# GRU, attention, RK4 and FP8 FFN on one core: small start loads, FFN input transposes in slot nine of sixteen, GpSimd's tail work on VectorE

## The reference

```python
def reference(x, cond, ...):
    h = gru(initial=cond, inputs=x, W_ih, W_hh, b_ih, b_hh)    # 64 steps, one after the other
    x = x + attention(layernorm(h) * gamma, Wq, Wkv, Wo)       # 16 heads of 128, one k/v head, rotary, causal
    q = rk4(q0=cond, p0=cond, drive=x, coupling, bias)         # 64 steps of 4 stages each
    return x + ffn(q, w_gate, w_up, w_down)                    # 512 -> 1408 -> 512, FP8 grid, row scales

def gru_cell(h, x):
    i_r, i_z, i_n = split(x @ W_ih + b_ih, 3)
    h_r, h_z, h_n = split(h @ W_hh + b_hh, 3)
    r, z = sigmoid(i_r + h_r), sigmoid(i_z + h_z)
    n = tanh(i_n + r * h_n)
    return (1 - z) * n + z * h

def derivative(q, p, drive):                                   # four of them to an RK4 step
    return q - q**3 / 3 - p + drive + tanh(q) @ coupling.T + bias, EPSILON * (q + ALPHA - BETA * p)
```

## Time and profile before

| | |
|---|---|
| median of three runs | 1656.17 us |
| the profiled execution, its own time | 1656.58 us |
| its span | 1654.7 us |
| mean granted TensorE clock | 0.978 of full |
| busy: TensorE, weight loads, VectorE, ScalarE, GpSimd | 90%, 56%, 68%, 35%, 24% |
| chain that ended last: TensorE, VectorE, idle, ScalarE, DMA, GpSimd | 74%, 11%, 6%, 5%, 2%, 2% |
| DMA, issue to landing: W_ih and W_hh (3 MB each) | 10.4 and 13.5 us |
| DMA, issue to landing: the first xT (64 KB), x rows (256 KB) | 1.8 and 2.7 us |

### The profile page before, as it was taken

One profiled execution on the slowest core, in us unless ns is written; L12 is line 12 of the kernel. 1 busy time (PEld: TensorE's weight loads), 2 busy tenths in 40 slices (PEclk: granted clock), 3 DMA queues, 4 the chain that ended last, 5 costly groups with the idle time before them and its releaser, 6 DMA issues.

```text
span 1654.7 us, 46345 instructions
## 1 busy us (share of the span) xinstructions
PE 1491.5 (90%) x16582; PEld 930.7 (56%) x16623; DVE 1122.2 (68%) x3561; ACT 587.3 (35%) x1902; POOL 400.2 (24%) x554
## 2 busy tenths in 40 slices
PE   5999999997699999999999996788888888888884
PEld 2333333336576766757576744566666666666652
DVE  2676777766674756556474714578888888888885
ACT  2444444541202021110202012445555555555552
POOL 0222211210000000000000001245555555555554
PEclk9999999998899999999999998999999999999997
DMA  7111112116000000000000032001111111111111
GB/s 293 47 51 46 44 49 73 57 26 175 1 1 26 0 25 2 24 6 19 25 0 25 0 127 102 24 27 36 36 37 33 33 32 35 32 37 42 35 34 33
DMA packets 90692, 72.44 MB, mean 44 GB/s; under 512 B 32472, under 2 KB 82824, under 8 KB 89608
## 3 DMA queue, kind: packets, MB, share of 16 engines
q1 hardware_dynamic: 71128, 59.38, 12.0%
q10 hardware_dynamic: 17744, 6.49, 1.6%
q0 software_dynamic: 1760, 5.77, 1.2%
HBM read 54.66 MB, written 16.94 MB: 43 GB/s over the span
## 4 chain that ended last, share of the span: by engine, by line
PE 74%; DVE 11%; issue 6%; ACT 5%; DMA 2%; POOL 2%; SPq 1%; DVEq 0%; POOLq 0%; ACTq 0%
PE ps L659 13%; PE ps L649 13%; PE ps L754 12%; PE ps L587 10%; PE ps L597 10%; PE ps L693 3%; PE ps L744 3%; PE ps L717 3%; ACT mem L962 2%; DVE mem L1283 2%; DVE mem L1325 2%; ACT ps L954 2%; PE ps L768 1%; PE ps L670 1%; DVE ps L1293 1%
## 5 line engine op out<-in xcount | busy, mean ns | idle before, releaser
L754 PE MATMUL ps<-mem 128*32 128x128 f32 x8192 | 282.1, 279 | 81.4 <-ACT mem L962 78.4
L754 PEld LDWEIGHTS ps<-mem 128*32 128x32 f32 x8192 | 214.3, 111 | 156.6 <-ACT mem L962 109.1
L649 PE MATMUL ps<-mem 128*128 128x512 f32 x512 | 224.6, 592 | 0.0
L659 PE MATMUL ps<-mem 128*128 128x256 f32 x1024 | 222.3, 379 | 0.0
L659 PEld LDWEIGHTS ps<-mem 128*128 128x128 f32 x1024 | 193.9, 190 | 26.0
L512 POOL TENSOR_TENSOR mem<-mem 128x128 f32<-128x128 f32 x64 | 30.9, 483 | 731.2 <-ACT mem L957 731.2
L587 PE MATMUL ps<-mem 128*32 128x384 f32 x2048 | 179.7, 492 | 0.7 <-DMA mem<-in_xT 0.7
L597 PE MATMUL ps<-mem 128*32 128x384 f32 x2048 | 177.6, 487 | 2.4 <-DVE mem L1110 2.4
L929 ACT ACTIVATE mem<-mem 128x512 f32<-128x512 f32 x32 | 19.7, 630 | 390.9 <-DVE mem L1223 390.9
L649 PEld LDWEIGHTS ps<-mem 128*128 128x128 f32 x512 | 95.6, 190 | 109.7 <-issue 109.3
L962 ACT ACTIVATE mem<-mem 128x64 f32<-128x64 f32 x512 | 102.7, 248 | 116.4 <-DVE mem L1283 116.3
(11 more groups left out here) (141 smaller groups left out, 2110.8 us busy)
## 6 DMA issues: line engine op xcount, KB each, us to landing
mem<-x_scr SPq DMA_DIRECT2D x128, 64.0 KB, 1.8
mem<-in_xT SPq DMA_DIRECT2D x64, 64.0 KB, 2.0
mem<-in_Wq SPq DMA_DIRECT2D x1, 4096.0 KB
mem<-in_Wo SPq DMA_DIRECT2D x1, 4096.0 KB, 20.8
mem<-in_x SPq DMA_DIRECT2D x16, 256.0 KB, 2.7
x_scr<-mem SPq DMA_DIRECT2D x32, 128.0 KB, 2.3
q_scr<-mem SPq DMA_DIRECT2D x64, 64.0 KB, 1.6
mem<-q_scr SPq DMA_DIRECT2D x64, 64.0 KB, 1.9
```

The source lines that it names most:

```text
L649: mm = pe.matmul(ps[:, 6 + pr, :], aoT[:, h, pr * P:pr * P + P], wo[:, h, :], start=(h == 0), stop=(h == HEADS - 1))
L659: mm = pe.matmul(ps[:, h % Q_BANKS, 0:BLK], wq[:, c, h * DH:(h + 1) * DH], xnb[:, c, :], start=(c == 0), stop=(c == NC - 1))
L754: mm = pe.matmul(ps[32 * j:32 * j + 32, st % 2, 0:P], thT[:, c, :], ct[:, c, j * P:(j + 1) * P], start=False, stop=(c == NC - 1), skip_gro ...
```

## The change

Start: the biases are prepared on the host for all 128 partitions and loaded by two DMAs on ScalarE's queue (256 and 128 KB). VectorE adds the second to two thirds of the first. TensorE makes one product into each of banks 0 and 1, ScalarE then writes the biases over them. SP loads xT, cond and the state first, waits for the bias loads, then loads W_ih and W_hh, the latter in two halves with a semaphore each. The copy of the identity on ScalarE moves behind the first pair of GRU steps.

Groups: TensorE's transposes of the FFN input move from slot 10 to slot 9 (the tenth).

Tail: in groups 16 to 18 VectorE does what GpSimd did, except for the gate's scale. The residual rows of tile 15 are loaded early into `qt`, its output is stored from `ysc`.

```diff
@@ sync
-            (five loads of biases and the selection matrix, b_ld)
             sp.dma_start(xt[0], ...); sp.dma_start(xt[1], ...); sp.dma_start(hT[1], ...); sp.dma_start(h_q[1], ...)
+            sp.wait_ge(b_ld, 32)
             sp.dma_start(wih, W_ih...).then_inc(wih_ld, 16)
-            sp.wait_ge(bias_split, 6)
-            for k in range(3):
-                sp.dma_start(bstack[NC * k:NC * k + NC, :], bparts[k][0:NC, :]).then_inc(stack_ld, 16)
-            sp.dma_start(whh, W_hh...).then_inc(whh_ld, 16)
+            for half, ld in enumerate(whh_ld):
+                rows = slice(2 * half, 2 * half + 2)
+                sp.dma_start(whh[:, rows, :], W_hh...[:, rows, :]).then_inc(ld, 16)
...
+            def last_x1():
+                sp.wait_ge(f_vq, PRIMED + NTILE)
+                for s in range(TILE_T):
+                    sp.dma_start(qt[32 * s:32 * s + 32, :]..., x1_scr[(NTILE - 1) * TILE_T + s]...).then_inc(x1_last, 16)
...
+                rows = ysc if isinstance(i, int) and i == NTILE - 1 else yout
...
             group(NTILE - 1, False, NTILE - 1 - LEAD, NTILE - LEAD)
+            last_x1()
             for i in range(NTILE - LEAD, NTILE):
-                group(None, False, i, i + 1 if i + 1 < NTILE else None)
+                group(None, False, i, i + 1 if i + 2 < NTILE else None)
@@ gpsimd, slot: each of these with "and rk"
-                    if k == 7:
+                    if k == 7 and rk:
-                    if k == 8:
+                    if k == 8 and rk:
-                    if k in (12, 15):
+                    if k in (12, 15) and rk:
-                if i is not None and k == 11:
+                if i is not None and k == 11 and rk:
@@ tensor
-            pe.wait_ge(stack_ld, 48)
-            pe.wait_ge(bias_split, 6)
+            pe.wait_ge(xt_ld[0], 16)
+            pe.wait_ge(bias_kept, 1)
+            for bank in range(2):
+                pe.matmul(ps[:, bank, :], xt[0]..., bias_bc, start=True, stop=True).then_inc(gate_bits, 1)
             pe.wait_ge(wih_ld, 16)
...
-                if prev:
-                    pe.wait_ge(gate_seed, t - 1)
-                else:
-                    pe.matmul(ps[:, par, :], sel_b[0:3 * NC, :], bstack[0:3 * NC, :], start=True, stop=False, ...)
+                pe.wait_ge(gate_seed, t + 1)
...
-            pe.matmul(ps[:, 4, :], sel_b[0:3 * NC, :], bstack[0:3 * NC, :], start=True, stop=True).then_inc(bias_mm, 1)
...
             pe.wait_ge(idb_done, 1)
             pair_of_steps(1)
...
-                    if k == 10:
+                    if k == 9:
                         pe.wait_ge(f_q8, i + 1)
                         (four transposes of qx8, f_qT)
@@ scalar
-            act.wait_ge(bias_mm, 1)
-            act.activation(bias_bc, ps[:, 4, :], ACT.Copy).then_inc(bias_kept, 1)
-            act.wait_ge(bias_kept, 1)
-            act.wait_ge(c_ld, 16 * N_CONST)
-            act.activation(id_b1, identf, ACT.Copy).then_inc(idb_done, 1)
+            for dst, src in ((bias_bc, gate_bias), (bias_hn, state_bias)):
+                act.dma_start(dst, src).then_inc(b_ld, 16)
+            for bank in range(2):
+                act.wait_ge(gate_bits, bank + 1)
+                act.activation(ps[:, bank, :], bias_bc, ACT.Copy).then_inc(gate_seed, 1)
...
             gru_pair(0)
+            act.wait_ge(c_ld, 16 * N_CONST)
+            act.activation(id_b1, identf, ACT.Copy).then_inc(idb_done, 1)
             gru_pair(1, lambda: scaled_rows(0, wraw, D))
@@ vector
-            (wait for b_ld, six operations that split the biases)
+            dve.wait_ge(b_ld, 32)
+            dve.tensor_tensor(bias_bc[:, P:3 * P], bias_bc[:, P:3 * P], bias_hn, ALU.add).then_inc(bias_kept, 1)
@@ vector, slot 7 of tile(0)
+                        if not rk:
+                            dve.wait_ge(f_xe, i + 1)
+                            dve.tensor_tensor(vq, vq, eq, ALU.add).then_inc(f_xa, 1)
+                            dve.wait_ge(f_xa, i + 1)
+                            dve.wait_ge(f_qT, i)
+                            dve.tensor_tensor(qx8, vq, eq, ALU.subtract).then_inc(f_q8, 1)
@@ vector, slot 11 of tile(1)
-                    if k == 15:
+                    if k == (15 if rk else 11):
                         t_added(v, 1)
+                    if k == 11 and not rk:
+                        for half in range(2):
+                            t_rounded(i, half)
@@ vector, slot 10 of tile(2), behind L1398
+                    if not rk:
+                        dve.wait_ge(f_ysc, i + 1)
+                        if i < NTILE - 1:
+                            dve.wait_ge(x1_ld, 16 * TILE_T * (i + 1))
+                            dve.wait_ge(o_wr, PRIMED + 16 * TILE_T * i)
+                            dve.tensor_tensor(yout, ysc, x1t, ALU.add).then_inc(f_out, 1)
+                        else:
+                            dve.wait_ge(x1_last, 16 * TILE_T)
+                            dve.tensor_tensor(ysc, ysc, qt, ALU.add).then_inc(f_out, 1)
```

More of the change, by code:

```diff
@@ L134, in take, with gru_attn_rk4_ffn @@
         return a
-def gru_attn_rk4_ffn(nc, xT, x, cond_quad, cond_T, W_ih, W_hh, bias_ih, bias_hh, sel, gamma, Wq, Wkv, Wo,
+def gru_attn_rk4_ffn(nc, xT, x, cond_quad, cond_T, W_ih, W_hh, gate_bias, state_bias, gamma, Wq, Wkv, Wo,
                      couplingT, bias_quad, w_gate, w_up, w_down, down_idx, ident, mean_of, trig, mask,
@@ L206, in gru_attn_rk4_ffn @@
         rh, npre, nval, zh, omz, nz = (f32(g.take(P), P) for _ in range(6))
[L207 to L214, removed]
+        bias_hn = f32(g.take(2 * P), 2 * P)
+        id_b1 = bf16(g.take(P // 2), P)
         part_mean, part_sq = f32(g.take(T), T), f32(g.take(T), T)
@@ L566, in group @@
                         p_step(4 * g + k // 4, k // 4, k % 4)
-                    slot(k, tile)
+                    slot(k, tile, rk)
             in_groups(pool, group)
@@ L593, in h_part @@
                 for c in range(NC):
+                    if c % 2 == 0 and first:
+                        pe.wait_ge(whh_ld[c // 2], 16)
                     if c % 2 == 0 and not first:
@@ L1338, in stage, with slot @@
                     dve.tensor_scalar(qn[s], dst, CLAMP, -CLAMP, ALU.min, ALU.max).then_inc(rk_qs, 1)
-            def slot(v, k, tile):
+            def slot(v, k, tile, rk):
                 if tile(2) is not None and k == 5:
@@ L1445, in group @@
                     if rk:
-                        stage(g, k // 4, k % 4, isinstance(g, int) and g == NTILE - 1, lambda: slot(v, k, tile))
+                        stage(g, k // 4, k % 4, isinstance(g, int) and g == NTILE - 1, lambda: slot(v, k, tile, rk))
                     else:
-                        slot(v, k, tile)
+                        slot(v, k, tile, rk)
                 if isinstance(g, int):
@@ L1473, in quad, with gate_rows @@
         return m.reshape(B, NC, P).transpose(1, 0, 2).reshape(P, P)
+    def gate_rows(bias, gate):
+        return quad(np.broadcast_to(bias.reshape(GATES, D)[gate], (B, D)))
     wih = a["L0_cond_W_ih"].reshape(D, GATES, D)[:, [2, 0, 1]].reshape(D, -1)
@@ L1524, in constants @@
     mask = np.where(j > i, -np.finfo(np.float32).max, 0).astype(np.float32)
-    sel = np.tile(np.repeat(np.eye(NC, dtype=np.float32), B, axis=1), (3, 1))
     mean_of = np.tile(np.eye(B, dtype=np.float32) / NC, (NC, NC))
-    return trig, mask, sel, mean_of
+    return trig, mask, mean_of
```

71 lines of the change are left out of this document (31 added, 40 removed).

## The result

The changed kernel took 1640.76 us (median of five runs, 1637.05 to 1644.43) beside 1654.91 for the kernel before: a ratio of 0.9907, 95% interval 0.9895 to 0.9918. The same program, timed again in a later job, gave 1643.52 (1641.33 to 1645.48) and 0.9917 (0.9904 to 0.993): 2.8 us higher in the median, with intervals that overlap. The profiled execution took 1640.76, with a span of 1638.8 and a mean granted clock of 0.976.

What follows compares the result with a forecast made beforehand. TensorE was taken as the GRU's bound, and ScalarE's waiting copy as what held up stage eleven's tanh. The terms -0.8 + 3.5 + 1.0 - 12.0 + 0.5 = -7.8 us gave 1648.4 us, range 1644.5 to 1653.

Steps and rivals of the forecast that it cites:

- The step that failed: Loop groups: with the transposes a slot earlier, stage eleven starts 0.77 us sooner a group, 9.2 us over twelve groups.
- Groups 0 to 2: Groups 1 and 2, like group 15, gain 0.9 to 1.0 us each from the moved transposes; group 0 has no copy.
- The start: Loads and first GRU steps: bias work -0.8, wait for the identity +3.5, slower clock +1.0 us.
- the bias work: Start, behind W_ih: the bias products removed from TensorE save about 0.8 us.
- the identity's copy: Before GRU input part 2: TensorE waits for ScalarE's later copy, 4.2 us less 0.71 of slack, +3.5 us.
- the clock behind the gap: After the idle gap before input part 2: products probably run at 1.2 GHz for some time, +1.0 us.
- +1.5 for this case: Same clock term at the start if the skill's throttling rule is taken as certain: +1.5 us rather than +1.0.
- The tail: Groups 16 to 18, VectorE doing GpSimd's work: later gate +1.9, then 0.8 and 0.6 sooner; +0.5 us, between -1.0 and +1.5.
- GpSimd was not late in slot nine: Rival: GpSimd delivers the FFN input late in slot nine, so groups gain nothing; +4.2 us, 1660.4; chance 0.05.
- it was the bound for stage ten alone: Rival: TensorE becomes the bound of stages nine to eleven, a group gains only 0.4 us; near -2, 1654; chance 0.07.
- The identity's wait: Rival at the start: the wait costs little, so the 3.5 and 1.0 us go; 1644; chance 0.08.
- The clock stays high: Case at the start: TensorE's clock doesn't drop in the gap; 1647.4 us, counted inside the forecast's own 0.80.

Runs made afterwards that it cites:

- e5_copy_later: The kernel before with only ScalarE's copy of the turned FFN input moved from slot 10 to slot 11, transposes left in slot 10: 1639.45 us, ratio 0.9902.
- e1_transposes: The kernel before with only the four transposes of the FFN input moved from slot 10 to slot 9: 1641.25 us, ratio 0.9912.
- e2_tail: The kernel before with only the tail's part of the change: 1655.68 us, ratio 0.9998.
- e3_start: The kernel before with only the start's part of the change, the identity's late copy included: 1658.79 us, ratio 1.0022.
- e4_ident: The changed kernel with ScalarE's copy of the identity back ahead of the first pair of GRU steps: 1638.26 us, ratio 0.9902.
- e6_undo_transposes: The changed kernel with the transposes back in slot 10, so new start and tail alone: 1657.51 us, ratio 1.0011.
- e7_undo_tail: The changed kernel with the old tail, so new start and transposes alone: 1645.27 us, ratio 0.9947.
- e8_best: The changed kernel with the identity's copy early, Wq loaded in four pieces and VectorE's tail rounding behind tile 15's gate: 1637.59 us, ratio 0.9884.
- e9_combined: The changed kernel with the identity's copy early, Wq in four pieces, transposes back in slot 10 and ScalarE's copy in slot 11: 1636.36 us, ratio 0.9874.
- e10_busy: The changed kernel with four extra unused 128x128 f32 products behind each stage of groups 0 to 2: 1657.95 us, ratio 1.0012.
- e11_after_again: The changed kernel, unaltered, timed and profiled again in a later job: 1643.52 us, ratio 0.9917.

## Why the prediction was wrong

The direction, the place and the mechanism were right; the largest term was sized too small, one term had the wrong sign, and one term was right by two errors that cancel.

Against the sum of -7.8 the two profiled spans differ by -15.9. By the table, the 8.1 us between them are: loop -12.1 for -9.2, 2.9 more; groups 0 to 2 -6.1 for -1.9, 4.2 more; tail -1.6 for +0.5, 2.1 more; start +4.6 for +3.7, 0.9 less; group 15 as forecast.

**The step that failed: "So stage eleven starts at 1184.9 instead of 1185.66: 0.77 a group."** Measured is 37.29 to 36.27, 1.02 a group, and 12.07 over the twelve (the first of them took 36.45). The step passed the transposes' 0.23 us on whole, first to stage ten's products and then "by the same distances" to VectorE's result. Neither holds:
- Stage ten's products came 0.14 later against stage nine's (2.17 to 2.31 over the groups; 2.30 in the one shown). Before, they stood 0.31 behind the start of the tanh (1182.15 to 1182.46), as those of stages nine and eleven do, which waited for it; so they too had waited for the tanh, and slot nine had a little room. Now it is 0.44 (1179.84 to 1180.28).
- VectorE's result came 0.04 later: 2.26 behind that of stage nine (1179.24 to 1181.50), before 2.22 (1181.56 to 1183.78). In both kernels VectorE's own work leads up to it without a gap, the leaving tile's scaling (L1398, now L1395) last, so the start of the products didn't set it. The lines of the kernel before, with the tanh:

```profile
1182.15 0.40 ACT L962 ACTIVATE mem<-mem 128x64 f32<-128x64 f32 x2
...
1183.11 0.75 DVE L1398 SCALAR_TENSOR_TENSOR mem<-ps,mem 128x512 f32<-128x512 f32 x1
```

- From there to stage eleven it is 0.92, not 0.90, and stage twelve follows 0.07 sooner (2.33 to 2.26), which I had not looked for.

0.77 + 0.19 - 0.02 + 0.07 = 1.01. e5_copy_later bears this out: with nothing moved on TensorE its result stays 2.22 behind, and its group is shorter by the same 0.04 (36.23 for 36.27). Over the twelve groups the step's miss is the loop's 2.9 us.

The other terms rest on the same table for the experiments' profiles:

| profile | to first stage | groups 0-2 | loop | group 15 | tail |
|---|---|---|---|---|---|
| e1_transposes | 1006.87 | 114.09 | 435.47 | 35.27 | 47.72 |
| e2_tail | 1006.55 | 116.90 | 447.45 | 36.49 | 47.17 |
| e3_start | 1011.39 | 114.97 | 447.74 | 36.52 | 47.31 |
| e4_ident | 1004.90 | 113.96 | 435.54 | 35.48 | 47.12 |
| e5_copy_later | 1007.17 | 110.93 | 434.76 | 35.42 | 47.85 |
| e6_undo_transposes | 1010.05 | 116.94 | 447.59 | 36.49 | 47.08 |
| e7_undo_tail | 1010.24 | 110.90 | 435.55 | 35.48 | 47.45 |
| e8_best | 1005.39 | 112.80 | 435.55 | 35.48 | 47.07 |
| e9_combined | 1004.52 | 113.83 | 434.93 | 35.43 | 47.64 |
| e10_busy | 1010.71 | 128.43 | 435.10 | 35.28 | 47.14 |
| e11_after_again | 1011.55 | 113.99 | 435.51 | 35.49 | 47.02 |

**Means instead of one pair.** Much of the rest of the 8.1 us is chance of the two executions. Over all profiles that share a part, the start costs 4.2 (1006.5 in four to 1010.7 in six, with the identity late), groups 0 to 2 give 3.7 (116.4 in four to 112.8 in six), the loop 12.1, group 15 1.0 and the tail 0.6 (47.8 in five to 47.2 in seven, e8_best's own order left out): 4.2 - 3.7 - 12.1 - 1.0 - 0.6 = -13.2, near the -13.7 and -15.4 of the two timings. Of the 5.4 us by which that differs from -7.8, the loop's 2.9 are the largest part, and the only one that stands in every profile alike.

**Groups 0 to 2** were put at 0.9 and 1.0, and at like clocks that was right (1.08 and 0.89); the rest is the clock. The 4.48 of group 2 in the kernel before was such a stretch, which I had named and then counted as 1.0. Whether the unblocked stages make low-clock stretches rarer, or whether the three profiles with 110.9 (after, e5, e7) are luck, stays open: e11_after_again has 113.99 with the same program as after.

**The start: +3.7 predicted, +3.70 measured at step 4 in this pair**, +3.6 for e3_start's time. Its terms, though, were not right. By the rows:
- the bias work: step 1's state part went from 28.83 to 26.79, -2.04 instead of -0.8. Part of this is chance too: the clock rose between 18 and 19 here and the first 64 products took 7.04, but 7.57 in e11_after_again. That state part starts at 28.59 on average in the four profiles with the old start and at 27.35 in the nine with the new one, -1.2;
- the identity's copy: from that state part to input part 2 it is 6.66 instead of 2.60, +4.06, less 0.90 that was waited for x at step 4: +3.2, where I had +3.5;
- the clock behind the gap: 5.12 from start to start instead of 2.58, +2.5, not +1.0. The granted clock was 0.79 over the gap and 0.50 (1.2 GHz) behind it.

-2.0 + 3.2 + 2.5 = +3.7: right by luck, since the bias work gave more and the gap cost more than I had. At the first RK4 stage the same two parts stand at 1004.9 on average without the identity's move (e4, e8, e9) and at 1010.7 with it: the move costs 5.7, and the rest of the new start gives 1.6. The rule of the Trainium skill that the prediction weighed ("TensorE: Matmul & The Clock Gate", section Why this matters for your kernels), a long gap between bursts throttles the matmul clock, was borne out behind the gap of 3.87 (0.50 granted). The prediction's +1.5 for this case was still one us short of the rows, and in two profiles a gap of 2.42 was enough (last section).

**The tail: +0.5 predicted, negative in the rows.** The first gate part came 2.34 late, where I had +3.0. GpSimd, now free, starts its scale 1.18 behind it (1610.03 to 1611.21); before, the gate stood 2.94 until GpSimd had finished L534 (1621.99 to 1624.93, both in the earlier trace rows). So 0.58 of the delay was left there, where I had 1.2, and 0.63 at tile 15's last scale, where I took 1.9. The kernel before was also late in this pair: its last scale stands 27.62 behind the last stage's products, 26.7 to 27.0 in the four other profiles with the old tail, and 27.4 to 28.5 in the seven with the new one. From that scale to the last transposes it is 8.67 in every profile with the old tail and 7.54 in every one with the new, 1.13 sooner where I had 0.8; the last add gives the 0.6 that I had; the rest of the 2.24 us saved behind the scale is the clock of the eleven down products, which take 3.8 to 4.9 us from one profile to the next. Alone, this part is worth less than two microseconds either way (e2_tail's interval); e7_undo_tail's median says more, and is not explained.

**The rivals.** GpSimd was not late in slot nine: 1.46 of slack. TensorE was idle 0.28 and 0.19 ahead of stages nine and eleven; of these three stages it was the bound for stage ten alone, where that cost the 0.14. The identity's wait cost all it was said to. "The clock stays high" was wrong here in both executions of the changed kernel that were profiled.

**What isn't explained.** The parts alone sum to 3.6 - 14.6 - 0.3 = -11.3 us; together they gave -15.4 and -13.7 in the two jobs (all by the ratios, times 1656). The differences, 4.1 and 2.4, are of the size by which one program's stretches of low clock vary, and each of these numbers has an interval of 1.5 to 2.2 us either way.

## What to carry to other kernels

- When an in-order engine waits for a late producer, ask not what the wait costs but what stands behind it. 2.05 us of waiting by a copy nobody needed soon put 1.02 us into every group, because the next tanh was queued behind it. Moving the waiting instruction one slot later is as good as moving its producer one slot earlier.
- Before passing a delay on through a chain, ask of each step who sets its time. The transposes put 0.23 us in front of stage ten's products; 0.14 arrived at the products and 0.04 at VectorE's result, because VectorE's own queue set it.
- An added gap on TensorE can cost the gap and slow work behind it: here 3.2 us and 2.5.
- Compare parts over several profiles. In one pair of them the start of the low and the full clock hid or doubled terms of one to four microseconds.

## What the runs showed of the hardware

- A gap of 2.41 to 2.43 us stands ahead of step 1's state part in eleven of the profiles. In nine of them the clock stayed high (32 products in 2.79); in e1_transposes and e5_copy_later, which have the kernel before's start unchanged, it dropped (4.48 in both):

```profile
27.88 4.48 PE L597 MATMUL ps<-mem 128*32 128x384 f32 x32 [2.42 <-DVE mem L1110]
```

  The gap of 3.85 to 3.87 was followed by slow products in all six profiles that have it, 5.26 to 5.35 in five and 4.32 in e6_undo_transposes.
- A granted clock of 1.00 at the very start of a trace isn't to be trusted. In the windows of the kernel before it stands at full while 32 products took 4.89, half speed; the products' own duration decides:

```profile
16.00:17.00 1.00, 1.00 (x8) 0.24 (x8) 0.00 (x0) 0.12 (x1) 0.00 (x0) 1.00 0.97 418
```

- VectorE and GpSimd take longer beside each other. VectorE's two additions took 2.75 beside GpSimd's work and 1.69 alone, its bits 3.02 and 0.95. By the Trainium skill ("GPSIMD Engine Reference", section Specifications) GpSimd's SBUF interfaces are shared with VectorE, with contention where VectorE has two SBUF inputs or runs in a mode with two ports; the additions, with two inputs, agree with that.
- A program's time with one stretch at low clock more or less moves by 3 us, as much as the smaller parts of this change are worth. They can be told only by their own intervals in several traces, not by the kernel's time.
